# Letting the row adds of one expert run together in the last group of a Mamba + mixture-of-experts kernel

## The chip, the cores and the metric

The kernel runs on one core of a Trainium2 chip. The metric is the device time of one execution in microseconds (us), the median of three executions. The core has five engines that run their own instruction streams and meet only at semaphores: TensorE (PE; its weight loads are shown as PEld), VectorE (DVE), ScalarE (ACT), GpSimd (POOL) and SyncE (SP), which here issues plain DMAs.

## The reference, cut to what matters

A Mamba block works on x of 8 x 1024 tokens of width 256, and then a mixture of 8 experts with the two best experts of each token:

```
logits = x_flat @ router_w + router_b
topk_weights, topk_indices = jax.lax.top_k(router_logits, k=2)
...
ff_gate = jax.lax.ragged_dot(sorted_tokens, we_gate, group_sizes)
ff_up = jax.lax.ragged_dot(sorted_tokens, we_up, group_sizes)
ff_out = jax.lax.ragged_dot(silu(ff_gate) * ff_up, we_down, group_sizes)
output_flat = jnp.zeros_like(x_flat).at[sorted_token_idx].add(ff_out * w)
```

A token stands in the lists of two experts, so two rows are added to its output row, and never two of the same expert.

## The kernel before

The tokens are worked through in 16 pieces of 512 (index q). The Mamba scan of a piece takes 16 slots of a loop over slots `s`, which every engine runs over in its own code. The router of piece q scatters each token's row twice into `sorted_x` in DRAM, which has a region for each expert. Rows are then taken back in tiles of 128 rows of one expert. There are 135 tiles (numbers v = 0 to 134) in 16 groups: 1 tile in the first, 8 in each of the others, and 22 in the last, which takes everything that is left. The last group is v = 113 to 134, and it runs after the scan has ended. Its k-th tile is v = 113 + k.

On the reference's inputs the router's choices fix what the last group holds. Counted from them: experts 0 to 6 have two tiles each, one with 128 rows and one with 44, 74, 29, 23, 10, 95 and 109 rows in this order (v = 113 and 114, 115 and 116, ..., 125 and 126); expert 7 has five full tiles (127 to 131); the last three (132 to 134) are empty and hold only rows with a number past the end of the output.

A late tile v goes through these steps, one slot apart or so: SP loads its 128 rows from `sorted_x` into `xt` (`load_tile`), PE transposes them (L740), ACT copies (`take_xt`, L1012), PE multiplies by gate and up weights (`late_gate_up`, L756), ACT takes a tanh (L1032), DVE makes the product (`activate`, L1235 and L1241), PE turns it (`late_turn`, L765), ACT copies it (`late_take`, L1026), PE multiplies by the down weights (`late_down`, L774), ACT scales the result into `yt` (`take_y`, L1020), and POOL issues an indirect DMA that adds the 128 rows to `out` in DRAM (`add_rows`, L1372). The order of the work on each engine is that of the code under the slot number: in slot s, PE has `late_down` of the tile of slot s-4, `late_turn` of s-3, `late_gate_up` of s-1 and the transpose of s; DVE has `activate` of s-2; POOL the add of s-5.

Semaphore `s_add` counts landed adds by 16. Three waits hang on it: `add_rows` of v waits until all earlier adds have landed; `take_y` of v waits until add v-2 has landed, since `yt` has two buffers (`NY`); `load_tile` of v waits until add v-7 has landed, since `xt` has seven (`NX`):

```
wait(pool, s_add, 16 * v)
wait(act, s_add, 16 * (v - NY + 1))
wait(sp, s_add, 16 * (v - NX + 1))
```

Of the kernel before, what the change touches and what calls it, by code (L numbers as in the profile page):

```python
# [24 lines left out]
J = P // 32  # L25
UN = CC * G
# [7 lines left out]
RW = DM + 2  # L34
NOWHERE = 4.0 * NQ * T
LAST = 3 * NE - 2
# [4 lines left out]
NX, NY = 7, 2  # L41
# [27 lines left out]
ALL = []  # L69
# [7 lines left out]
for g in ALL:  # L77
    for k in range(g.nk):
        assert g.at[k] not in BEGINS and g.at[k] > max(BEGINS, default=-99)
        BEGINS[g.at[k]] = g, k  # L80
TOTAL_SLOTS = ALL[-1].at[-1] + 9


def scattered(s):
# [3 lines left out]
def tiles_in(s, late=None):  # L88

    return [BEGINS[s]] if s in BEGINS and late in (None, s >= LATE_FROM) else []  # L90
# [85 lines left out]
def mamba_moe(nc, x, w_in, w_xp, w_dt, w_out, w_moe, chan, a_log, ln_gb, r_w, r_b, consts, out):  # L176
    with ExitStack() as ctx:
        def sb(name, shape, dt=F32):
            return ctx.enter_context(nc.sbuf_tensor(name, shape, dt))
# [4 lines left out]
        def sem(name):  # L184
            return ctx.enter_context(nc.semaphore(name))
# [20 lines left out]
        REPS = 9222  # L206
# [73 lines left out]
        te = sb("te", [P, 3, LAST], U32)  # L280
        tb = sb("tb", [P, 3, LAST], U32)
        te_pad = sb("te_pad", [P, NE], U32)


        xt = sb("xt", [P, NX, RW])
        xT = sb("xT", [P, 2, DC, P])
        yt = sb("yt", [P, NY, DM])
        th = sb("th", [P, 2, DC, P])
        hT = sb("hT", [P, 2, DC, P])
        hT2 = b_bc[:, 0:2, 0:DM].rearrange("p b (c t) -> p b c t", t=P)  # L290
# [83 lines left out]
        s_ga = sem("s_ga")  # L374
        s_h = sem("s_h")
        s_add = sem("s_add")
        s_token = sem("s_token")
        s_none = sem("s_none")
        s_state = sem("s_state")
# [8 lines left out]
        def wait(eng, s, value):  # L388
            if value > 0:
                eng.wait_ge(s, value)  # L390

        def by_parity(v):

# [22 lines left out]
        def _(sp):  # L416
# [63 lines left out]
            def load_tile(g, k):  # L480
                v = g.tiles + k
                if k == 0:
                    scattered_all(sp, 0, g.q)
                    scattered_all(sp, 1, g.q)
                    sp.wait_ge(s_te, g.q + 1)
                    if g.q == NQ - 1:
                        sp.wait_ge(s_zero, 16 * (NE + 1))
                wait(sp, s_add, 16 * (v - NX + 1))
                at = tile_row(sp, g, k)
                sp.dma_start(xt[:, v % NX, :], sorted_x[bass.ds(at, P), :]).then_inc(s_xt[v % NX], 16)  # L490


            chosen = {}
# [87 lines left out]
        def _(pe):  # L581
# [150 lines left out]
            def late_transpose(g, k):  # L732
                v = g.tiles + k
                pe.wait_ge(s_xt[v % NX], 16 * (v // NX + 1))
                if v == LATE:
                    pe.wait_ge(s_m2, UN * NQ)
                    pe.wait_ge(s_h3, UN * NQ)
                wait(pe, s_xv, v - 1)
                for c in range(DC):
                    last = pe.transpose(dA[:, 2 + v % 2, c * P:(c + 1) * P], xt[:, v % NX, c * P:(c + 1) * P], ident)  # L740
                last.then_inc(s_ta, 1)


# [63 lines left out]
        def _(act):  # L807
# [206 lines left out]
            def take_y(g, k):  # L1014
                v = g.tiles + k
                act.wait_ge(s_td, v + 1)
                if v < LATE:
                    wait(act, s_ta, TOKENS_WITH[v])
                wait(act, s_add, 16 * (v - NY + 1))
                act.activation(yt[:, v % NY, :], p_a[:, DM:2 * DM], ACT.Copy, scale=xt[:, v % NX, DM:DM + 1]).then_inc(s_yv, 1)  # L1020

            def late_take(g, k):
                v = g.tiles + k
# [69 lines left out]
        def _(dve):  # L1093
# [86 lines left out]
            def place(q):  # L1180
# [38 lines left out]
                j = step_of(dve.tensor_tensor(taken[:], some[:, 1:NE + 1], some[:, 0:NE], ALU.subtract))  # L1219
                dve.wait_ge(s_place, i)  # L1220
                dve.wait_ge(s_past, q + 1)
                k = step_of(dve.tensor_tensor(past[:, 0:nk], past[:, 0:nk], step[:].unsqueeze(1).to_broadcast([P, nk, NE + 2]), ALU.mult))
                dve.wait_ge(s_place, j)
                dve.scalar_tensor_tensor(r5[:, QT + 1, :], taken[:], -float(P), r5[:, QT + 1, :], ALU.mult, ALU.add).then_inc(s_state, 1)
                dve.tensor_copy(te[:, g.b, 0:nk], tef[:, 0:nk])
                dve.wait_ge(s_place, k)
                m = step_of(dve.tensor_reduce(tbf[:, 0:nk], past[:, 0:nk], AX_X, ALU.add))
                dve.wait_ge(s_place, m)
                dve.tensor_scalar(tb[:, g.b, 0:nk], tbf[:, 0:nk], float(ZERO_PAGE), None, ALU.min).then_inc(s_te, 1)
                assert done[0] == PL * (q + 1)  # L1230

            def activate(g, k):
                v = g.tiles + k
                dve.wait_ge(s_tanh, v + 1)
                dve.scalar_tensor_tensor(th[:, v % 2], th[:, v % 2], 1.0, gate(g, v), ALU.add, ALU.mult).then_inc(s_ga, 1)  # L1235
                dve.wait_ge(s_ga, v + 1)
                if v < LATE + 2:
                    wait(dve, s_td, v - 1)
                else:
                    dve.wait_ge(s_turn, v - LATE - 1)  # L1240
                dve.tensor_tensor(hT[:, v % 2], th[:, v % 2], up(g, v), ALU.mult).then_inc(s_h, 1)  # L1241

            for s in range(FIRST, TOTAL_SLOTS):
                q, n = s // UN, s % UN
                unit = 0 <= s < UN * NQ
                tail = 0 <= q - 1 < NQ
                if unit:
                    unit_first(s)
                if unit:
                    unit_third(s)  # L1250
                for p in range(NQ):
                    if s == UN * (p + 1) + 8:
                        weights(p)
                        place(p)
                if unit:
                    unit_second(s)
                for g, k in tiles_in(s - 2):
                    activate(g, k)
                if unit:
                    unit_last(s)  # L1260
                if unit and n in (4, 8, 12):
                    gated(q, n // G - 1)
                if tail and n == 0:
                    gated(q - 1, CC - 1)
                if n == 6 and tail:
                    route(q - 1)
                if s == FIRST + 4:
                    tables()

        @block.gpsimd  # L1270
        def _(pool):
# [93 lines left out]
            def add_rows(g, k):  # L1365

                v = g.tiles + k
                pool.wait_ge(s_yv, v + 1)
                pool.wait_ge(s_x2w, 16 * (g.q + 1))
                wait(pool, s_add, 16 * v)  # L1370
                number = xt[:, v % NX, DM + 1:DM + 2].bitcast(U32)
                pool.indirect_dma_start(out=out_rows, out_offset=bass.IndirectOffsetOnAxis(ap=number, axis=0), in_=yt[:, v % NY, :], in_offset=None,  # L1372
                                        bounds_check=NQ * T - 1, oob_is_err=False, compute_op=ALU.add).then_inc(s_add, 16)

            def no_token():
# [90 lines left out]
```

## Time and profile before

| | us |
|---|---|
| median of 3 runs | 2319.36 (2318.93 to 2322.07) |
| profiled execution, its own time | 2327.84 |
| its span in the profile | 2325.9 |
| from the start of add 113 to the start of add 134 | 93.5 |
| granted TensorE clock over the span, as a share of 2.4 GHz | 0.888 |

A row of the timeline has the start of an instruction from the start of the span, its length, engine, line, operation and tiles, and in brackets how long the engine had stood idle and what the profile takes for the releaser. For a DMA, the POOL row is the making of the transfer's descriptors; the chain of waits shows how long it took from there to its landing ("DMA out<-yt,xt").

### The profile page before, as it was taken

How to read it: one execution, taken by the hardware profiler on the slowest of the kernel's cores; microseconds unless marked ns; L12 is line 12 of the kernel's file. 1: busy time of each engine (PE TensorE's matmuls, PEld its weight loads, DVE VectorE, ACT ScalarE, POOL GpSimd, SP SyncE). 2: the span in 40 equal slices, each digit the busy share in tenths (PEclk: the TensorE clock that was granted, in tenths of full speed). 3: DMA queues.
4: the chain of work that ended last, by engine and by line, in shares of the span. 5: the costliest groups of instructions: out<-in, count | busy, mean ns of one | idle time of the engine just before them, and what ended most of it. 6: DMA issues, size and time to landing. Idle time of an engine off the chain costs nothing.

```text
span 2325.9 us, 32531 instructions
## 1 busy us (share of the span) xinstructions
PE 1795.3 (77%) x7694; PEld 923.0 (40%) x7694; DVE 1893.7 (81%) x2437; ACT 1806.5 (78%) x3753; POOL 1933.7 (83%) x1190
## 2 busy tenths in 40 slices
PE   5566768697878788797878788797878788666785
PEld 2112323153534344353434444353434344343542
DVE  0389988899889888899889888899889888999221
ACT  5888888888898788888998788888998787763332
POOL 1588897989999898999999898999999898987333
PEclk9888978797989898998989898997989898786998
DMA  1635454477777786677777786677777786797332
GB/s 57 145 83 141 105 141 109 125 177 184 169 178 178 169 213 160 170 183 184 174 175 180 163 218 157 171 183 180 176 179 178 160 221 147 183 259 221 70 49 34
DMA packets 217979, 369.34 MB, mean 159 GB/s; under 512 B 31040, under 2 KB 86592, under 8 KB 217664
## 3 DMA queue, kind: packets, MB, share of 16 engines
q1 hardware_dynamic: 192208, 333.56, 58.1%
q0 software_dynamic: 25584, 33.71, 7.5%
q8 instruction: 65, 1.06, 0.2%
q14 instruction: 122, 1.00, 0.1%
HBM read 285.05 MB, written 83.01 MB: 158 GB/s over the span
## 4 chain that ended last, share of the span: by engine, by line
issue 23%; POOL 23%; ACT 18%; PE 18%; DVE 9%; DMA 8%; POOLq 0%; ACTq 0%; DVEq 0%; SPq 0%
DMA out<-yt,xt 8%; POOL arena L1324 8%; DVE dA L1116 5%; PE ring L603 5%; ACT dA L979 4%; POOL arena L1332 4%; POOL out L1372 3%; POOL sorted_x L1362 2%; PE yps L697 2%; PE ring L611 2%; DVE arena L1116 2%; POOL arena L1347 2%; POOL arena L1342 1%; PE p_g L729 1%; PE ring L640 1%
## 5 line engine op out<-in xcount | busy, mean ns | idle before, releaser
L1324 POOL TENSOR_TENSOR arena<-arena,b_bc 128x2048 f32<-128x2048 f32 x256 | 998.4, 3900 | 88.3 <-PE yps L697 88.3
L979 ACT ACTIVATE dA<-arena,a_s 128x512 f32<-128x512 f32 x1024 | 680.5, 684 | 116.0 <-DVE arena L1125 69.9
L1116 DVE TENSOR_TENSOR_SCAN dA<-dA,arena 128x512 f32<-128x512 f32 x384 | 454.5, 1213 | 156.8 <-ACT dA L979 107.3
L1116 DVE TENSOR_TENSOR_SCAN dA<-dA,carry,arena 128x512 f32<-128x512 f32 x384 | 477.6, 1274 | 52.3 <-POOL arena L1324 36.2
L697 PE MATMUL yps<-arena,const_s 128*32 128x512 f32 x2048 | 320.4, 702 | 59.9 <-POOL arena L1332 35.9
L1332 POOL TENSOR_TENSOR arena<-arena,c_bc 128x511 f32<-128x511 f32 (+1 forms) x256 | 335.0, 1308 | 28.3 <-DVE arena L1116 26.5
L1125 DVE TENSOR_TENSOR arena<-dA,c_bc 128x1024 f32<-128x1024 f32 x256 | 313.6, 1225 | 8.8
L1372 POOL DMA_INDIRECT out<-yt,xt x135 | 215.0, 1592 | 115.7 <-ACT yt L1020 84.1
L595 PE MATMUL ring<-arena 128*128 128x512 f32 x488 | 265.4, 670 | 55.5 <-ACT arena L883 21.6
L729 PEld LDWEIGHTS p_g<-xT,w_e 128*128 128x128 f32 x1680 | 216.7, 209 | 127.5 <-issue 127.5
L603 PE MATMUL ring<-arena 128*128 128x512 f32 x480 | 236.8, 639 | 35.3 <-ACT arena L883 13.6
L729 PE MATMUL p_g<-xT,w_e 128*128 128x128 f32 x1680 | 236.7, 299 | 20.8 <-issue 11.4
L709 PE MATMUL p_a<-w_e,hT 128*128 128x256 f32 x420 | 128.3, 434 | 112.0 <-ACT xT L1012 80.6
L1138 DVE TENSOR_TENSOR arena<-dA,c_bc 128x512 f32<-128x512 f32 x256 | 176.4, 689 | 5.2
L1116 DVE TENSOR_TENSOR_SCAN arena<-dA,carry,arena 128x512 f32<-128x512 f32 x128 | 163.2, 1275 | 11.3 <-ACT dA L979 11.3
L1116 DVE TENSOR_TENSOR_SCAN arena<-dA,arena 128x512 f32<-128x512 f32 x128 | 155.2, 1213 | 20.6 <-ACT dA L979 20.6
L1362 POOL DMA_INDIRECT sorted_x<-xf,pos x128 | 127.1, 993 | 45.3 <-issue 30.1
L595 PEld LDWEIGHTS ring<-arena 128*128 128x128 f32 x488 | 91.5, 208 | 183.5 <-issue 88.2
L603 PEld LDWEIGHTS ring<-arena 128*128 128x128 f32 x480 | 91.2, 200 | 161.4 <-issue 95.9
L709 PEld LDWEIGHTS p_a<-w_e,hT 128*128 128x128 f32 x420 | 86.0, 216 | 160.4 <-issue 114.6
L697 PEld LDWEIGHTS yps<-arena,const_s 128*32 128x32 f32 x2048 | 43.5, 115 | 229.8 <-issue 177.7
L623 PE MATMUL ring<-w_out_s,sz 128*128 128x256 f32 x512 | 122.7, 382 | 4.7 <-ACT uc L887 3.8
(171 smaller groups left out, 2973.5 us busy)
## 6 DMA issues: line engine op xcount, KB each, us to landing
arena<-dt_d SPq DMA_DIRECT2D x512, 256.0 KB
w_e<-in_w_moe SPq DMA_DIRECT2D x105, 512.0 KB, 4.7
dt_d<-arena SPq DMA_DIRECT2D x128, 256.0 KB, 2.4
w_e<-in_w_moe SPq DMA_DIRECT2D x105, 256.0 KB
xt<-sorted_x SPq DMA_DIRECT2D x135, 129.0 KB
b_bc<-bc_d SPq DMA_DIRECT2D x256, 64.0 KB, 2.4
c_bc<-bc_d SPq DMA_DIRECT2D x256, 64.0 KB, 5.3
xs<-in_x SPq DMA_DIRECT2D x16, 512.0 KB, 4.4
```

Source lines behind the costliest of these rows:

```text
L595: last = pe.matmul(bank(q, name), w_in_s[:, c, ch * P:(ch + 1) * P], xnT[:, c, :], start=c == 0, stop=c == DC - 1)
L603: last = pe.matmul(bank(q, f"W{c}"), d_conv[:, c, k, :], ubuf[:, c % 2, k:k + T], start=k == 0, stop=k == TAPS - 1)
L697: last = pe.matmul(yps[32 * j:32 * j + 32, :], sumsel, hs[:, u % 3, j, :], start=False, stop=g == G - 1, skip_group_check=True)
L709: last = pe.matmul(p_a[:, DM:2 * DM], hT[:, v % 2, c, :], w_e[:, v % 2, col:col + DM], start=c == 0, stop=c == DC - 1)
L729: last = pe.matmul(p_g[:, f, :], w_e[:, v % 2, col:col + P], xT[:, v % 2, c, :], start=c == 0, stop=c == DC - 1)
L979: act.activation(dA[:, j, :], rep_dt[:, c % 2, j, :], ACT.Exp, scale=a_s[:, n, j:j + 1]).then_inc(s_exp, 1)
L1116: return dve.tensor_tensor_scan(out_ap, dA[:, j, :], hs[:, u % 3, j, :], init, ALU.mult, ALU.add)
L1125: dve.tensor_tensor(hs[:, u % 3, 0:2], dA[:, 0:2], c_bc[:, g, :].unsqueeze(1).to_broadcast([P, 2, T]), ALU.mult).then_inc(s_m01, 1)
L1138: dve.tensor_tensor(hs[:, u % 3, 2], dA[:, 2], c_bc[:, g, :], ALU.mult).then_inc(s_m2, 1)
L1324: pool.tensor_tensor(hs[:, u % 3], rep_dtu[:, c % 2], b_bc[:, g, :].unsqueeze(1).to_broadcast([P, J, T]), ALU.mult).then_inc(s_dbu, 1)
L1332: pool.tensor_tensor(hs[:, u % 3, 3, 0:end], hs[:, u % 3, 3, 0:end], c_bc[:, g, 0:end], ALU.mult).then_inc(s_hp, 1)
L1372: pool.indirect_dma_start(out=out_rows, out_offset=bass.IndirectOffsetOnAxis(ap=number, axis=0), in_=yt[:, v % NY, :], in_offset=None, bou ...
```

## The change

For v < 113 nothing changes. For the last group: the rows go into 15 new buffers (`xt_own`) and then into the seven of `xt`, the results into 22 new buffers (`yt_own`), both in parts of `arena` that the scan has left; the loads no longer wait for adds, except that the sixteenth waits once for add 112; `take_y` no longer waits for adds. When the tile table of the last group is made, DVE makes `turn` too: for tile k, 16 times the number of adds up to the first tile of its expert. Before the add of tile k > 0, DVE reads its entry into a register, waits until `s_add` has reached it, and lets POOL go through `s_go`, by a copy of one column. So adds of one expert wait only for the adds up to their expert's first tile.

```diff
+OWN = ALL[-1].tiles
+NEW_ROWS = 15
...
+        def rows_of(v):
+            k = v - OWN
+            return xt[:, v % NX, :] if k < 0 else xt_own[:, k, :] if k < NEW_ROWS else xt[:, k - NEW_ROWS, :]
+
+        def result_of(v):
+            return yt[:, v % NY, :] if v < OWN else yt_own[:, v - OWN, :]
...
-                wait(sp, s_add, 16 * (v - NX + 1))
+                if v < OWN:
+                    wait(sp, s_add, 16 * (v - NX + 1))
+                elif k == 0:
+                    sp.wait_ge(s_dbu, UN * NQ)
+                    sp.wait_ge(s_exp, J * UN * NQ)
+                elif k == NEW_ROWS:
+                    sp.wait_ge(s_add, 16 * OWN)
+                if v >= OWN:
+                    sp.wait_ge(s_xt[v % NX], 16 * (v // NX))
...
-                wait(act, s_add, 16 * (v - NY + 1))
-                act.activation(yt[:, v % NY, :], p_a[:, DM:2 * DM], ACT.Copy, scale=xt[:, v % NX, DM:DM + 1]).then_inc(s_yv, 1)
+                if v < OWN:
+                    wait(act, s_add, 16 * (v - NY + 1))
+                elif k == 0:
+                    act.wait_ge(s_ymm, UN * NQ)
+                act.activation(result_of(v), p_a[:, DM:2 * DM], ACT.Copy, scale=rows_of(v)[:, DM:DM + 1]).then_inc(s_yv, 1)
...
+                if last:
+                    dve.tensor_tensor(past[:, :, 1:NE + 1], past[:, :, 1:NE + 1],
+                                      count_e[:, 1:NE + 1].unsqueeze(1).to_broadcast([P, LAST, NE]), ALU.mult).then_inc(s_order, 1)
+                    dve.wait_ge(s_order, 1)
+                    dve.tensor_reduce(turnf, past[:, :, 1:NE + 1], AX_X, ALU.add).then_inc(s_order, 1)
+                    dve.wait_ge(s_order, 2)
+                    dve.tensor_scalar(turn[:], turnf, 16.0, 16.0 * OWN, ALU.mult, ALU.add).then_inc(s_order, 1)
+
+            def may_add(k):
+
+                if k == 1:
+                    dve.wait_ge(s_order, 3)
+                dve.wait_ge(s_add, dve.value_load(turn[0:1, k:k + 1], min_val=16 * OWN, max_val=16 * TILES))
+                dve.tensor_copy(past2[:, k, 0:1], turnf[:, k:k + 1]).then_inc(s_go, 1)
...
+                for g, k in tiles_in(s - 5, True):
+                    if g.tiles == OWN and k > 0:
+                        may_add(k)
...
-                wait(pool, s_add, 16 * v)
-                number = xt[:, v % NX, DM + 1:DM + 2].bitcast(U32)
-                pool.indirect_dma_start(out=out_rows, out_offset=bass.IndirectOffsetOnAxis(ap=number, axis=0), in_=yt[:, v % NY, :], in_offset=None,
+                if v <= OWN:
+                    wait(pool, s_add, 16 * v)
+                else:
+                    pool.wait_ge(s_go, k)
+                number = rows_of(v)[:, DM + 1:DM + 2].bitcast(U32)
+                pool.indirect_dma_start(out=out_rows, out_offset=bass.IndirectOffsetOnAxis(ap=number, axis=0), in_=result_of(v), in_offset=None,
```

On DVE, in the slots of the last group, there were only the two instructions of `activate` for one tile after another (number, line, operation, and the semaphores it waits for):

```order
2028 L1235 SCALAR_TENSOR_TENSOR th<-th,p_g 128x256 [waits s_tanh]
2029 L1241 TENSOR_TENSOR hT<-th,p_g 128x256 [waits s_turn,s_ga]
2030 L1235 SCALAR_TENSOR_TENSOR th<-th,yps 128x256 [waits s_tanh]
2031 L1241 TENSOR_TENSOR hT<-th,yps 128x256 [waits s_turn,s_ga]
2032 L1235 SCALAR_TENSOR_TENSOR th<-th,p_g 128x256 [waits s_tanh]
2033 L1241 TENSOR_TENSOR hT<-th,p_g 128x256 [waits s_turn,s_ga]
```

Now, from the slot of tile 117's `activate` on (2005 and 2006), a register load, two register operations and a copy of one column stand behind each `activate`; the copy waits for `s_add`:

```order
2005 L1285 SCALAR_TENSOR_TENSOR th<-th,yps 128x256 [waits s_tanh]
2006 L1291 TENSOR_TENSOR hT<-th,yps 128x256 [waits s_turn,s_ga]
2007 L1279 TENSOR_LOAD turn [waits s_order]
2008 L1279 ISA x2
2009 L1280 COPY arena<-arena 128x1 [waits s_add]
2010 L1285 SCALAR_TENSOR_TENSOR th<-th,p_g 128x256 [waits s_tanh]
2011 L1291 TENSOR_TENSOR hT<-th,p_g 128x256 [waits s_turn,s_ga]
2012 L1279 TENSOR_LOAD turn
2013 L1279 ISA x2
2014 L1280 COPY arena<-arena 128x1 [waits s_add]
```

The copy for the add of tile v stands behind `activate` of tile v+3 and ahead of `activate` of tile v+4.

On POOL the end of the program was this, with the eight scatters of piece 15 between the adds of group 14; 27 adds stand at its end, the last five of group 14 and the 22 of the last group:

```order
1094 L1372 DMA out_0<-yt,xt 8192x256 [waits s_add,s_x2w,s_yv] x2
1095 L1362 DMA sorted_x<-xf,pos 66688x258 [waits s_token,s_zero,s_w12,s_pos] x4
1096 L1372 DMA out_0<-yt,xt 8192x256 [waits s_add,s_x2w,s_yv]
1097 L1362 DMA sorted_x<-xf,pos 66688x258 [waits s_swap,s_token,s_zero,s_w12,s_pos] x4
1098 L1372 DMA out_0<-yt,xt 8192x256 [waits s_add,s_x2w,s_yv] x27
```

and is now:

```order
1097 L1415 DMA sorted_x<-xf,pos 66688x258 [waits s_swap,s_token,s_zero,s_w12,s_pos] x4
1098 L1428 DMA out_0<-yt,xt 8192x256 [waits s_add,s_x2w,s_yv] x5
1099 L1428 DMA out_0<-arena 8192x256 [waits s_add,s_x2w,s_yv]
1100 L1428 DMA out_0<-arena 8192x256 [waits s_go,s_x2w,s_yv] x14
1101 L1428 DMA out_0<-arena,xt 8192x256 [waits s_go,s_x2w,s_yv] x7
```

Add 113 still waits for `s_add`; 114 to 134 wait for `s_go`. The order of the adds is the same.

On SP the loads of the last group each waited for `s_add`; now the first (tile 113) waits for the scatters, the table and the scan's end, and each of the next 14 only for the landing of the load seven before it:

```order
1823 L499 TENSOR_LOAD tb [waits s_dbu,s_zero,s_exp,s_te,s_xt1,s_sct11,s_sct01]
1824 L499 ISA x2
1825 L519 ISA
1826 L519 DMA arena<-sorted_x 128x258
1827 L499 TENSOR_LOAD tb [waits s_xt2]
1828 L499 ISA x2
1829 L519 ISA
1830 L519 DMA arena<-sorted_x 128x258
1831 L499 TENSOR_LOAD tb [waits s_xt3]
```

So 15 loads of the last group can be issued one behind the other.

## Rows read from the trace of the kernel before

**Rows 1.** Windows: busy time of each engine, granted clock, DMA share, GB/s.

```profile
2215.00:2228.00 13.00, 12.66 (x51) 7.78 (x51) 3.99 (x10) 5.91 (x18) 3.09 (x2) 1.00 0.32 48
2228.00:2318.00 90.00, 61.33 (x212) 34.65 (x210) 14.53 (x35) 25.62 (x72) 30.84 (x20) 0.92 0.28 43
```

**Rows 2.** The chain of waits: adds of the last group and what stands between them.

```profile
2203.18 3.77 DMA out<-yt,xt
...
2224.82 3.78 DMA out<-yt,xt
2228.68 0.48 ACT yt L1020
...
2229.45 3.65 DMA out<-yt,xt
...
2239.15 3.68 DMA out<-yt,xt
...
2243.69 4.10 DMA out<-yt,xt
...
2248.64 3.06 DMA out<-yt,xt
...
2311.26 2.70 DMA out<-yt,xt
```

**Rows 3.** Timeline of POOL: add 107, behind a scatter, then adds 112, 115, 127 and 134.

```profile
2190.88 1.60 POOL L1372 DMA_INDIRECT out<-yt,xt  x1 [0.30 <-issue]
...
2220.20 1.55 POOL L1372 DMA_INDIRECT out<-yt,xt  x1 [6.14 <-ACT yt L1020]
...
2233.96 1.54 POOL L1372 DMA_INDIRECT out<-yt,xt  x1 [2.96 <-ACT yt L1020]
...
2287.99 1.54 POOL L1372 DMA_INDIRECT out<-yt,xt  x1 [2.98 <-ACT yt L1020]
...
2318.35 1.54 POOL L1372 DMA_INDIRECT out<-yt,xt  x1 [2.00 <-DMA out<-yt,xt]
```

**Rows 4.** Timeline of ACT: results of tiles 111 and 112, tanh of 115 and 117.

```profile
2207.03 0.47 ACT L1020 ACTIVATE yt<-p_a,xt 128x256 f32<-128x256 f32 x1 [4.17 <-DMA out<-yt,xt]
2207.41 0.38 ACT L1012 ACTIVATE xT<-dA 128x256 f32<-128x256 f32 x1
...
2218.95 0.47 ACT L1020 ACTIVATE yt<-p_a,xt 128x256 f32<-128x256 f32 x1
...
2220.89 0.38 ACT L1032 ACTIVATE th<-yps 128x256 f32<-128x256 f32 x1
...
2226.93 0.38 ACT L1032 ACTIVATE th<-yps 128x256 f32<-128x256 f32 x1
```

**Rows 5.** Timeline of DVE: a small cast, and `activate` of tile 115.

```profile
2184.82 0.16 DVE L1205 CAST pos<-posf 128x8 uint32<-128x8 f32 x1
...
2221.30 0.42 DVE L1235 SCALAR_TENSOR_TENSOR th<-th,yps 128x256 f32<-128x256 f32 x1 [2.15 <-ACT th L1032]
2221.75 0.42 DVE L1241 TENSOR_TENSOR hT<-th,yps 128x256 f32<-128x256 f32 x1
```

**Rows 6.** Timeline of PE: the turning of tile 115.

```profile
2224.30 0.38 PE L765 MATMUL dA<-const_s,hT 128*128 128x128 f32 x2
```

**Rows 7.** One tile load of SP, step by step (ns min/median/max).

```profile
L478 SPq TENSOR_LOAD <-tb x28: 269/274/681, 2165.0 to 2291.9; - x28
L478 SPq FUSED_REGOPS  x28: 152/152/156, 2165.3 to 2292.2; - x28
...
L490 SPq DMA_DIRECT2D xt<-sorted_x x22: 215/338/347, 2200.5 to 2292.6; - x22
```

**Rows 8.** Chain of waits, and window, of one add beside the scan's traffic.

```profile
1126.58 5.90 DMA out<-yt,xt
...
1126.00:1132.00 6.00, 6.00 (x33) 4.25 (x32) 5.44 (x5) 5.51 (x13) 5.85 (x5) 1.00 1.09 222
```

**Rows 9.** DMA queue of SP from 2206 to 2212 us (packets, MB, share of 16 engines): one tile load.

```profile
q1 hardware_dynamic: 144, 0.13, 8.4%
```

More of the change, by code:

```diff
@@ L282, in mamba_moe @@
         te_pad = sb("te_pad", [P, NE], U32)
+        turn = sb("turn", [P, LAST], U32)
         xt = sb("xt", [P, NX, RW])
@@ L287, in mamba_moe @@
         yt = sb("yt", [P, NY, DM])
+        FREE = 6 * DM * NE
+        xt_own = lies(FREE, NEW_ROWS, RW)
+        past2 = lies(FREE + NEW_ROWS * RW, LAST, NE + 2)
+        turnf = lies(FREE + NEW_ROWS * RW + LAST * (NE + 2), LAST)
+        yt_own = lies(REPS + 4 * J * T, LAST, DM)
+        assert FREE + NEW_ROWS * RW + LAST * (NE + 3) <= REPS + 4 * J * T and LAST * DM <= 3 * J * T
         th = sb("th", [P, 2, DC, P])
@@ L376, in mamba_moe @@
         s_add = sem("s_add")
+        s_order = sem("s_order")
+        s_go = sem("s_go")
         s_token = sem("s_token")
@@ L487, in load_tile @@
                         sp.wait_ge(s_zero, 16 * (NE + 1))
-                wait(sp, s_add, 16 * (v - NX + 1))
+                if v < OWN:
[7 more added lines that the diff above has]
+                    sp.wait_ge(s_xt[v % NX], 16 * (v // NX))
                 at = tile_row(sp, g, k)
-                sp.dma_start(xt[:, v % NX, :], sorted_x[bass.ds(at, P), :]).then_inc(s_xt[v % NX], 16)
+                sp.dma_start(rows_of(v), sorted_x[bass.ds(at, P), :]).then_inc(s_xt[v % NX], 16)
             chosen = {}
@@ L739, in late_transpose @@
                 for c in range(DC):
-                    last = pe.transpose(dA[:, 2 + v % 2, c * P:(c + 1) * P], xt[:, v % NX, c * P:(c + 1) * P], ident)
+                    last = pe.transpose(dA[:, 2 + v % 2, c * P:(c + 1) * P], rows_of(v)[:, c * P:(c + 1) * P], ident)
                 last.then_inc(s_ta, 1)
@@ L1221, in place @@
                 dve.wait_ge(s_past, q + 1)
-                k = step_of(dve.tensor_tensor(past[:, 0:nk], past[:, 0:nk], step[:].unsqueeze(1).to_broadcast([P, nk, NE + 2]), ALU.mult))
+                starts = past2 if last else past
+                if last:
+                    dve.wait_ge(s_dbu, UN * NQ)
+                    dve.wait_ge(s_exp, J * UN * NQ)
+                k = step_of(dve.tensor_tensor(starts[:, 0:nk], past[:, 0:nk], step[:].unsqueeze(1).to_broadcast([P, nk, NE + 2]), ALU.mult))
                 dve.wait_ge(s_place, j)
@@ L1226, in place @@
                 dve.wait_ge(s_place, k)
-                m = step_of(dve.tensor_reduce(tbf[:, 0:nk], past[:, 0:nk], AX_X, ALU.add))
+                m = step_of(dve.tensor_reduce(tbf[:, 0:nk], starts[:, 0:nk], AX_X, ALU.add))
                 dve.wait_ge(s_place, m)
@@ L1230, in place @@
                 assert done[0] == PL * (q + 1)
+                if last:
+                    dve.tensor_tensor(past[:, :, 1:NE + 1], past[:, :, 1:NE + 1],
[9 more added lines that the diff above has]
+                dve.tensor_copy(past2[:, k, 0:1], turnf[:, k:k + 1]).then_inc(s_go, 1)
             def activate(g, k):
```

## The prediction, made before the changed kernel ran

> **What bounds the kernel now.** I read the windows first. From 2215 to 2228 us the last group's tiles flow with PE busy for 12.66 of 13 us; from 2228 to 2318 no engine is full (PE 61.33 of 90, DVE 14.53) and the DMA engines are busy for 0.28 of the time [rows 1]. So something serial holds the last 90 us. The chain of waits names it: it runs from one add's landing to the next [rows 2]. Add 113 starts at 2224.82 and lands 3.78 later, at 2228.60; add 114 starts at 2229.45, 0.85 later. The ACT row at 2228.68 between them is a bystander: it is `take_y` of tile 115, which had waited for the same landing. It gives one useful price, 0.08 us from a landing to the next instruction of a waiting engine. One tile costs about 3.7 + 0.85 us, and from add 115 to add 127 twelve tiles took 2287.99 - 2233.96 = 54.03 us [rows 3], 4.5 each.
>
> The next limit below it is PE. Undisturbed, the tanh of tiles 115 and 117 start at 2220.89 and 2226.93 [rows 4]: 3.02 us a tile. What 3.02 instead of 4.5 would save at most over 21 adds is some 31 us.
>
> **The change, part by part.** Before add 113 nothing in the order of adds changes, and add 113 still waits for add 112. From then on there are two regimes.
>
> *Prices.* From a landing to the next expert's first add the way is now landing, DVE's copy, POOL: 0.08, a copy of one column, and POOL's reaction. For the copy I take the small cast's 0.16 [rows 5]. POOL's reaction is 0.78, from `take_y` of tile 112 (2218.95 + 0.47) to its add at 2220.20 [rows 3, 4]. The sum is 1.02, instead of 0.85: the new link costs 0.17 at each boundary. A second add of the same expert needs only POOL: 1.54 for the descriptors and the 0.30 that stands ahead of an unhindered indirect DMA, 1.84 [rows 3]. DVE is quicker than that: two instructions of `activate`, 0.87 [rows 5], a register load with its operations, 0.27 + 0.15 by SP's rows [rows 7], and the copy, 1.6 in all. DVE's own register load is in no row; its bounds are nothing, where it is hidden, and SP's longest, 0.68.
>
> *The pairs, tiles 114 to 126.* Add 114's permission stands behind `activate` of tile 117. That starts 0.41 after its tanh (2220.89 to 2221.30 for tile 115 [rows 4, 5]), at 2227.34; with 0.87, 0.42, 0.16 and 0.78 the add starts at 2229.6, and before at 2229.45: the same, and I keep 2229.45. It lands 3.65 later. Add 115, the first of expert 1, follows at 2234.12. Then each pair costs 1.84 to its second add, that one's landing, and 1.02. The landings are 3.68 for 116, and I take this for 124 and 126 too, and 3.06 for 118, with 29 rows, and for 120 and 122 [rows 2]. Six pairs: 6 x 2.86 + 3 x 3.68 + 3 x 3.06 = 37.38, so add 127 starts at 2271.50 instead of 2287.99. The first add of a pair starts 1.84 earlier and lands within 4.10, the longest row [rows 2], so mostly earlier than the second.
>
> *Is DVE's wait in the way of the tiles behind it?* This is the cost to look for: `may_add` of tile v blocks `activate` of v+4. Undisturbed, `activate` of tile 115 ends at 2222.17 [rows 5] and PE turns the tile at 2224.30 [rows 6]: 2.1 us of slack. Undisturbed, `activate` of tile v starts at 2227.34 + 3.02 x (v - 117). For 121 that is 2239.4, and the permission before it comes at 2239.9; for 131 it is 2269.6, and the permission comes at 2270.7, 1.1 late. All the others lie between. So no blocked `activate` uses up the slack, and PE keeps its 3.02. If boundaries were dearer by more than about 0.2 us each, the slack would be gone at the end of the pairs, and every further 1 us would be 1 us of the result.
>
> *Expert 7 and the empty tiles.* Now the compute leads: add 128 stands behind `activate` of tile 132, which ends at 2227.34 + 15 x 3.02 + 0.87 = 2273.5; with 0.42, 0.16 and 0.78, add 128 starts at 2274.9. Then 129 at 2277.9, 130 at 2280.9. No `activate` is left, so 131 follows by 1.84 at 2282.8 and lands at 2286.6 (3.78). The three empty tiles wait for it: 132 at 2287.6, 133 and 134 by 1.84 each, 134 at 2291.3. It lands in 2.70, as an empty tile does [rows 2], at 2294.0. Before, that was 2318.35 + 2.70 = 2321.05. **This part is worth 27.0 us.**
>
> *The loads.* Tile loads leave the adds behind and come in one burst: 15 loads, one every 0.77 us by SP's steps [rows 7], from 2200.5 to about 2212, and each takes 8.4% of 6 us, 0.5 us, of every DMA engine [rows 9]. In this burst lie adds 108 (2198.41) and 109 (2203.18 [rows 2]); add 109's landing frees ACT for the result of tile 111 at 2207.03, behind which tile 112's copy at 2207.41 stands [rows 4], and with it the start of the whole group. Beside the scan's traffic, with the DMA engines full, an add took 5.90 instead of 3.77 [rows 8]. The burst fills 0.5/0.77 of the engines and the adds need some of the rest, so it is nearer to full than to empty only for part of the time; bounds are 0 and 2 x 2.1 = 4.2, and I take 0.8. Later loads meet little. The burst's gain, rows that are there earlier, is nothing: PE waits for no rows worth naming here.
>
> The Trainium skill ("DMA: Bandwidth & Descriptors", section "Queues, rings and completion order") says that a DMA's semaphore increment lands only after all earlier writes of that DMA engine, across its queues, so a landing would also wait for load writes queued before it. The trace's 5.90 agrees in direction [rows 8]; the sum would take the upper bound, 4.2, instead of 0.8.
>
> *The rest at nothing.* The three table instructions on DVE (under 1 us) run at about 2187, ahead of an `activate` whose result PE doesn't want for 2 us; if that cover were gone they would cost at most that 1 us, once. The waits for `s_dbu`, `s_exp` and `s_ymm` are for the scan, which has ended. The copies of one column queue ahead of `activate` only.
>
> The same skill (same page, section "Latency and other measured facts") gives about 600 ns as the floor of a `tensor_load`; SP's rows show 0.27 [rows 7], so the trace disagrees. By the page DVE's step would be 0.33 longer: still under POOL's 1.84 in a pair, and 0.33 once for expert 7.
>
> **The sum.** 27.0 - 0.8 = 26.2 us. The profiled execution took 2327.84 and would take 2301.6; the median stands 8.5 us lower, and I take the difference over: 2319.36 - 26.2 = 2293.2.
>
> **The rivals.**
> - *Slower landings side by side* (0.20). No row before shows two adds in flight. If the second one's transfer queued behind the first's, it would land later by what an add takes after its descriptors, some 2.1 less the 0.3 by which it starts later: 1.8. Six pairs cost 10.8 more, of which the slack still absorbs 1.0: gain 26.2 - 9.8 = 16.4, or 2303.0. With 4.2 from the burst it is 13.0. For it speaks [rows 8]; against it, that the DMA engines stand idle for 0.72 of this time [rows 1] and that the adds of a pair are 1.84 apart.
> - *The change doesn't do what it says* (0.04): in effect one add at a time, for instance because DVE's order lets a second permission out only when its pair's landing has passed. Then 21 steps cost 0.17 more each: +3.6 us, 2323, within 0.2%. Against it: DVE needs only 1.6 us between two permissions.
> - *Slower* (0.04): two adds in flight hinder each other in DRAM so much that a pair is dearer than serial. A pair costs 9.0 now (54.03/6); 1.84 + landing + 1.02 passes it once the second add's landing is over 6.1 us. At 8.0, pairs cost 10.9, 11 us more over six; the run of expert 7 and the empties, 30.4 us from add 127 to 134 before, would still save about 6: 5 us slower, 2324. The longest landing in this stretch is 4.10 [rows 2].
> - *As forecast* (0.72): its own range is a gain of 23 to 28, 2291 to 2296.
>
> **How the numbers follow.** The range runs from 2290, with the burst at nothing and a tile or two quicker, to 2303, the first rival's time; beyond lie its worse half and the two last cases. About 0.2% (4.6 us) is what a measurement can tell from no change. Faster 0.92 (the forecast and the first rival), same 0.04, slower 0.04.
>
> **What would show it.** In the profile after: adds of a pair 1.9 us apart and the next pair's first about 1.0 after the landing; add 127 near 2272, 128 to 130 spaced by 3.0, the last add near 2292; the chain of waits through DVE's L1280 in the pairs and through PE in expert 7; `take_y` waiting for PE only. The prediction is wrong if PE waits for DVE's product in the pairs (slack overdrawn), if landings of second adds are over 4 us, or if the row of tile 112's copy moves from 2207.4 to later than 2209.

## The result, and the profile after

The changed kernel took 2297.94 us (median of 4 runs) against 2320.72 before; the ratio is 0.9887, with a 95% interval of 0.9864 to 0.9909. By the interval that is a gain of 21 to 32 us; the two medians differ by 22.8. Predicted were 26.2 and 2293.2 us. The profiled execution's span is 2297.1 us instead of 2325.9. (One of the six executions of the repeat below took 5806.81 us, for a reason that no run shows; its ratio leaves this one out.)

The adds first, in the timeline of POOL after the change (columns as in [rows 3]). The rows are adds 113 to 119, then 127 to 132, and 134; L1428 is the indirect DMA of `add_rows`:

```profile
2224.17 1.54 POOL L1428 DMA_INDIRECT out<-arena  x1 [3.08 <-DMA out<-yt,xt]
2229.07 1.54 POOL L1428 DMA_INDIRECT out<-arena  x1 [3.36 <-DVE arena L1280]
2233.82 1.54 POOL L1428 DMA_INDIRECT out<-arena  x1 [3.21 <-DVE arena L1280]
2235.67 1.54 POOL L1428 DMA_INDIRECT out<-arena  x1 [0.30 <-issue]
2241.63 1.54 POOL L1428 DMA_INDIRECT out<-arena  x1 [4.42 <-DVE arena L1280]
2243.47 1.54 POOL L1428 DMA_INDIRECT out<-arena  x1 [0.30 <-issue]
2247.64 1.54 POOL L1428 DMA_INDIRECT out<-arena  x1 [2.62 <-DVE arena L1280]
...
2272.60 1.54 POOL L1428 DMA_INDIRECT out<-arena  x1 [3.14 <-DVE arena L1280]
2274.44 1.54 POOL L1428 DMA_INDIRECT out<-arena,xt  x1 [0.30 <-DVE arena L1280]
2276.29 1.54 POOL L1428 DMA_INDIRECT out<-arena,xt  x1 [0.30 <-issue]
2278.46 1.54 POOL L1428 DMA_INDIRECT out<-arena,xt  x1 [0.63 <-issue]
2280.99 1.54 POOL L1428 DMA_INDIRECT out<-arena,xt  x1 [0.99 <-ACT arena L1052]
2285.84 1.54 POOL L1428 DMA_INDIRECT out<-arena,xt  x1 [3.30 <-DVE arena L1280]
...
2289.53 1.54 POOL L1428 DMA_INDIRECT out<-arena,xt  x1 [0.30 <-issue]
```

A pair is now visible as a pair: 2233.82 and 2235.67, with "0.30 <-issue" ahead of the second, which waited for nothing. The first add of the next expert has DVE's copy (L1280) as its releaser. From add 113 to add 134 it is 65.36 us; before it was 93.53 [rows 2, 3].

On DVE the permission for add 119, the first of expert 3, and then `activate` of tile 123, which had stood blocked behind it, and the permission for the pair's second add:

```profile
2246.62 0.15 DVE L1280 COPY arena<-arena 128x1 f32<-128x1 f32 x1 [3.92 <-DMA out<-arena]
2246.69 0.41 DVE L1285 SCALAR_TENSOR_TENSOR th<-th,yps 128x256 f32<-128x256 f32 x1
2247.13 0.42 DVE L1291 TENSOR_TENSOR hT<-th,yps 128x256 f32<-128x256 f32 x1
2247.77 0.16 DVE L1280 COPY arena<-arena 128x1 f32<-128x1 f32 x1 [0.21 <-issue]
```

From the copy's start to the add at 2247.64 it is 1.02 us, and with 0.08 from the landing 1.10. The second permission comes 1.15 behind the first, well under POOL's 1.84, and the register load (L1279; ns min/median/max) is nearly as short as SP's [rows 7]:

```profile
L1279 DVEq TENSOR_LOAD <-turn x21: 296/303/542, 2227.2 to 2285.5; - x21
```

The chain of waits has turned over. Before, it went from landing to landing [rows 2]. After, the profile follows PE from tile 112 on, one turning, gate and up multiplication, transpose and down multiplication behind the other, and meets the adds only at add 131 (start, length, what):

```profile
2206.66 0.38 ACT xT L1041
...
2276.71 1.72 PE p_g L785 x4
2278.43 0.86 PE p_a L803 x4
2279.29 0.23 PE dA L794 x2
...
2279.83 0.48 ACT arena L1052
2280.30 0.69 issue
2280.99 3.80 DMA out<-arena,xt
...
2284.82 0.15 DVE arena L1280
```

The link into add 131 has to be read with care. The profile names the ACT row that came last before it, 2279.83, but that is the result of tile 132. Results that read `xt` (of tiles 128 and later) start at 2267.20, so the fourth of them, tile 131's, is the row at 2277.03, which ended 3.5 us ahead of the add. What add 131 waited for is its permission: the copy at 2279.97 stands behind `activate` of tile 134, and the add follows it by 1.02 us, as at every boundary. In the repeat below it is 1.02 too (2268.29 and 2269.31).

```profile
2267.20 0.47 ACT L1052 ACTIVATE arena<-p_a,xt 128x256 f32<-128x256 f32 x1
...
2277.03 0.47 ACT L1052 ACTIVATE arena<-p_a,xt 128x256 f32<-128x256 f32 x1
...
2279.83 0.47 ACT L1052 ACTIVATE arena<-p_a,xt 128x256 f32<-128x256 f32 x1
```

```profile
2279.34 0.42 DVE L1291 TENSOR_TENSOR hT<-th,p_g 128x256 f32<-128x256 f32 x1
2279.97 0.15 DVE L1280 COPY arena<-arena 128x1 f32<-128x1 f32 x1 [0.22 <-DMA out<-arena,xt]
```

`activate` of tile 134 in its turn waits for PE and the tanh. So the end of the last group is now paced by compute, through DVE's place in the order, and the add chain of the pairs runs beside it, nearly as long. The windows say the same: PE is busy for 57.44 of 66 us, where it was 61.33 of 90 [rows 1].

```profile
2224.00:2290.00 66.00, 57.44 (x225) 34.89 (x223) 18.10 (x59) 27.02 (x76) 32.86 (x22) 0.98 0.33 45
```

### The profile page after: what moved, and what is told of

Same layout as the page of the kernel before. It is cut to its first block, busy times and chain, and to the rows that moved or that the text cites. A ratio compares the mean times of both kernels' runs of the same rounds, so it can differ in the third digit from the quotient of the medians.

```text
span 2297.1 us, 32600 instructions
## 1 busy us (share of the span) xinstructions
PE 1789.8 (78%) x7694; PEld 921.0 (40%) x7694; DVE 1896.2 (83%) x2461; ACT 1807.2 (79%) x3753; POOL 1933.9 (84%) x1190
## 4 chain that ended last, share of the span: by engine, by line
PE 24%; issue 22%; POOL 21%; ACT 20%; DVE 8%; DMA 4%; POOLq 0%; ACTq 0%; DVEq 0%; SPq 0%
POOL arena L1377 6%; ACT dA L1008 5%; POOL arena L1385 4%; DVE dA L1148 4%; PE ring L632 4%; DMA out<-yt,xt 3%; PE ring L624 3%; POOL out L1428 3%; PE yps L726 3%; POOL sorted_x L1415 2%; PE ring L640 2%; DVE arena L1148 2%; POOL arena L1400 2%; ACT L1008 1%; ACT L945 1%
## 5 line engine op out<-in xcount | busy, mean ns | idle before, releaser
L1428 POOL DMA_INDIRECT out<-yt,xt x113 | 181.0, 1602 | 55.1 <-ACT yt L1052 28.2
```

## The experiments

Executions of one kernel scatter by some 10 to 15 us here, and so does the time at which add 113 starts (2213.8 to 2226.8 us in these profiles, though the kernels are all but the same up to there). So I read each profile by stretches of the add chain, and take the clock's ratio beside it. Times are the starts of the adds on POOL, in us; each row is one profiled execution:

| kernel | 109 to 113 | 113 to 115 | 115 to 127 | 127 to 134 | 113 to 134 | ratio to before (95%) |
|---|---|---|---|---|---|---|
| before | 21.64 | 9.14 | 54.03 | 30.36 | 93.53 | |
| changed | 22.11 | 9.65 | 38.78 | 16.93 | 65.36 | 0.9887 (0.9864 to 0.9909) |
| again | 21.97 | 9.44 | 37.71 | 16.73 | 63.88 | 0.9865 (0.9839 to 0.9891) |
| own_serial | 21.75 | 9.70 | 53.59 | 30.38 | 93.67 | 0.9998 (0.9984 to 1.0013) |
| one_at_a_time | 21.70 | 10.10 | 56.98 | 31.52 | 98.60 | 1.0026 (1.0011 to 1.0041) |
| static_table | 21.85 | 6.77 | 36.28 | 17.96 | 61.01 | 0.9872 (0.9850 to 0.9894) |
| sp_permits | 21.99 | 6.41 | 38.84 | 16.07 | 61.32 | 0.9866 (0.9844 to 0.9888) |
| earlier | 21.77 | 7.00 | 37.93 | 17.27 | 62.20 | 0.9865 (0.9840 to 0.9890) |
| later | 21.66 | 12.56 | 38.91 | 15.94 | 67.41 | 0.9887 (0.9860 to 0.9913) |
| paced_loads | 21.65 | 10.00 | 38.14 | 16.79 | 64.93 | 0.9885 (0.9861 to 0.9909) |
| dear_permit | 21.85 | 11.28 | 40.63 | 17.86 | 69.77 | 0.9906 (0.9884 to 0.9929) |
| empties | 21.69 | 9.39 | 37.24 | 14.44 | 61.07 | 0.9852 (0.9825 to 0.9879) |
| sp_empties | 23.57 | 6.40 | 38.54 | 14.95 | 59.89 | 0.9849 (0.9824 to 0.9874) |

**again.** The changed kernel once more, with no edit.

> The changed kernel once more, to narrow its gain. The two traces stand 28.8 us apart in their spans, the medians 22.8. If the traces show all of it, five more rounds give a gain of 26 to 29 us; if the new kernel is slower when it isn't profiled, the gain stays near 23.

2293.62 against 2324.52 us, a gain of 30.9, and by the interval 25 to 37. That is somewhat above the 26 to 29 that were expected if the traces showed all of it. The stretches of the two profiles show gains of 28.2 and 29.7 us from add 113 to 134, so the first 22.8 was low by scatter of the total, as far as the overlapping intervals can tell. The second profile is 1.5 us shorter from add 113 to 134, and 1.3 us of this has a cause that the trace shows: in the first, PE stood still three times behind a late permission (see "DVE's block and PE's slack" below).

**own_serial.** The buffers without the concurrency:

```diff
-                if v <= OWN:
-                    wait(pool, s_add, 16 * v)
-                else:
-                    pool.wait_ge(s_go, k)
+                wait(pool, s_add, 16 * v)
...
-                for g, k in tiles_in(s - 5, True):
-                    if g.tiles == OWN and k > 0:
-                        may_add(k)
```

> The buffers alone: own row and result buffers and unhindered loads, but every add waits for all earlier ones, and no permissions. Theory (the adds' own chain was the bound, not the buffers): no change against the kernel before, within 0.2%; the adds stay 4.5 us apart. Rival (the waits of take_y and of the loads were part of the chain): up to 5 us faster.

No change, 0.9998, and the same 93.67 us. The buffers and the freed waits of `take_y` and the loads are worth nothing by themselves: the ACT rows in the chain before [rows 2] were bystanders. The whole gain is the adds' own chain. No run lets adds run together without the own buffers, so it isn't shown whether they are needed for it.

**one_at_a_time.** The detour without the concurrency:

```diff
-                dve.wait_ge(s_add, dve.value_load(turn[0:1, k:k + 1], min_val=16 * OWN, max_val=16 * TILES))
+                dve.wait_ge(s_add, 16 * (OWN + k))
```

> Permissions through DVE, but each add waits for all earlier ones. It prices the detour alone. Theory: 0.17 us more for each of 21 adds than in the kernel before, 97 us from add 113 to add 134, and 3 to 4 us slower than before, or no change by the clock. Rival (blocked activates stall PE on top): over 100 us.

98.60 us, 4.9 more than with `own_serial`, or 0.23 for each of 21 adds, and slower than before by 0.1 to 0.4%. Expected were 97 us, the rival had over 100. So the detour itself costs, and somewhat more than the 0.17 that was reckoned. Its chain of landings is so long that DVE's blocked `activate` does reach PE here (who waited for whom, us in total, times, longest):

```profile
PE dA L794 <- DVE hT L1291: 13.4, 15, 2.2
```

That is 13.4 us of PE's time, but PE was not the bound here, and the detour's price explains the longer stretch without it. The changed kernel's own list has no such row; its blocked `activate` reaches PE in another way, told below.

**static_table.** POOL waits on constants and DVE is out of it:

```diff
+FIRST_OF = [0, 0, 2, 2, 4, 4, 6, 6, 8, 8, 10, 10, 12, 12, 14, 14, 14, 14, 14, 19, 19, 19]
...
-                    pool.wait_ge(s_go, k)
+                    pool.wait_ge(s_add, 16 * (OWN + FIRST_OF[k]))
...
-                for g, k in tiles_in(s - 5, True):
-                    if g.tiles == OWN and k > 0:
-                        may_add(k)
```

> POOL waits on constants, the table worked out beforehand for these inputs; DVE gives no permissions and is never blocked. Theory (DVE's place in the order sets the start of the pairs and of the last adds): add 114 starts about 3 us earlier, near 1.84 behind add 113; a boundary costs 0.85 instead of 1.0; PE has no gaps left, and the end is set by the result of tile 131, so the last add starts some 1.5 us earlier than in the changed kernel. Rival (DVE's detour costs the whole chain): 3 us at the start and 0.15 at each of 7 boundaries reach the end, 4 us.

Add 114 follows 113 by 1.84 us, where it was 4.90 in both profiles of the changed kernel:

```profile
2217.51 1.54 POOL L1426 DMA_INDIRECT out<-arena  x1 [3.15 <-DMA out<-yt,xt]
2219.35 1.54 POOL L1426 DMA_INDIRECT out<-arena  x1 [0.30 <-issue]
```

The pairs take 36.28 us, 1.4 less than with "again": six boundaries at 0.24 less. That is the detour's price again, by another way. But of the 4.1 us gained by add 127 only 2.9 are left at add 134 (61.01 against 63.88), since add 131 now waits for the result of tile 131, which doesn't come sooner: it starts 52.71 us behind add 113, instead of 55.55 behind the permission in "again". The theory had this limit right and its worth wrong: it reckoned with 1.5 us, as if add 131 of the changed kernel waited for its result too. Against the first profile (65.36) the gain is 4.35, so by the number alone the rival's 4 isn't out; it is out by the 1.2 us that are lost between add 127 and the end.

**sp_permits.** The same permissions with the table made on the chip, but given by SP:

```diff
+            def sp_may_add(k):
+                if k == 1:
+                    sp.wait_ge(s_order, 3)
+                sp.wait_ge(s_add, sp.value_load(turn[0:1, k:k + 1], min_val=16 * OWN, max_val=16 * TILES))
+                sp.sem_inc(s_go, 1)
```

Its calls stand behind SP's loads of the slot, and those of `may_add` on DVE are left out.

> SP, idle at the end but for the loads, reads the table and gives the permissions, between the loads; DVE gives none. Theory (the detour is cheap, its place on DVE is what costs): as with the table of constants, 61 us from add 113 to add 134 instead of 64 to 65, add 114 within 2.5 us of add 113, a boundary at 0.9 to 1.1. Rival (the register load and the wait for a register are dear wherever they stand): 64 us or more.

61.32 us, as with the constants; expected was 61. Add 131 starts 52.90 us behind add 113, set by its result as in static_table. So what is dear isn't the table but where the permission stands. The pairs alone took 38.84 us, 2.6 more than with the constants; most of this stands at two adds, 116 and 124, whose landings were late (5.54 and 5.32 us to the next add, where the kernels with DVE's permissions mostly have 4.7), and it was gone by add 131.

**earlier** and **later.** The permission one slot sooner (behind `activate` of v+2), or one slot later:

```diff
-                for g, k in tiles_in(s - 5, True):
+                for g, k in tiles_in(s - 4, True):
...
-                for g, k in tiles_in(s - 5, True):
+                for g, k in tiles_in(s - 6, True):
```

> Each permission one slot earlier on DVE, behind activate of tile v+2 and ahead of v+3. Theory (slack of 2.1 us): add 114 starts 3 us earlier; but a blocked activate is now needed 3 us sooner, so PE waits some 1 to 2 us at each boundary and gives the 3 us back: 62 to 67 us from add 113 to 134, with PE waiting for DVE's product at most boundaries. Rival (blocking never matters): 61 us, as with the constants.

> Each permission one slot later on DVE, behind activate of tile v+4. Theory (place in DVE's order counts): add 114 starts 3.0 us later, the pairs follow shifted by that, add 130 stands behind the last activate and 131 1.84 behind it; the last add starts 2.5 to 3.5 us later than in the changed kernel. Rival (landings alone pace the adds): the same as the changed kernel within 1 us, since DVE is idle for most of the time.

Later came out nearly as expected: add 115 starts 2.9 to 3.1 us later, add 134 2.1 to 3.5. Earlier was a miss in part. Add 114 starts 1.85 behind 113, as expected, and 62.20 us lies in the expected range, but PE doesn't stand still at most boundaries, only at two; its row for the gaps ahead of the gate multiplication is this (the second number is how often):

```profile
PE p_g L785 <- issue: 0.4, 2, 0.3
```

By the starts of the tanh the two gaps cost 0.95 us together, and not 1 to 2 at each boundary. I had overlooked that the landings move with the permission: add 115 starts 2.4 to 2.7 us sooner too, so in the pairs the blocked `activate` is hardly nearer to its deadline than before.

**paced_loads.** No burst of loads:

```diff
                 if v >= OWN:
                     sp.wait_ge(s_xt[v % NX], 16 * (v // NX))
+                    sp.wait_ge(s_xv, v - 3)
```

> The changed kernel with no burst: a load of the last group waits until three tiles before it are taken by ACT. Theory (the burst costs little): add 109 lands in 3.8 instead of 4.15 us, add 116 in 3.7 instead of 4.9; the last add 0 to 1.5 us earlier, not told by the clock. Rival (the burst holds back the start by up to 4.2 us, the prediction's bound): 3 to 4 us faster than the changed kernel.

Add 109 lands in 3.85 instead of 4.15 us, each from its own chain of waits (paced_loads first, then the changed kernel):

```profile
2205.10 3.85 DMA out<-yt,xt
```

```profile
2202.06 4.15 DMA out<-yt,xt
```

From add 109 to add 113 it takes 21.65 us, as it did before (21.64); the kernels with the burst took 21.66 to 22.11, but for sp_empties, which has its own reason (below). So the burst costs 0 to 0.5 us, not 0.8, and by far not 4.2. Add 116 was expected to land in 3.7 us and took 3.9. The last add came 0.4 us sooner than in the first profile of the changed kernel and 1.0 later than in the second, which two profiles can't tell from no change. So the rival's 3 to 4 us are out.

**dear_permit.** One more pass of DVE ahead of each permission:

```diff
+                dve.tensor_scalar(t_s[:], t_s[:], 1.0, None, ALU.mult).then_inc(s_order, 1)
+                dve.wait_ge(s_order, 3 + k)
                 dve.tensor_copy(past2[:, k, 0:1], turnf[:, k:k + 1]).then_inc(s_go, 1)
```

> Ahead of every permission DVE passes once over a tile of 128x512 (its values unchanged), some 0.3 to 0.7 us. Theory (the pairs are a chain, the expert run is not): each of seven boundaries is that much dearer, and nearly all of it reaches the end, since PE's slack is used up by then: 67 to 69 us from add 113 to add 134. Rival (the compute behind PE sets the end, landings are hidden): 65 us, as in the changed kernel.

The pass takes 0.43 us (ns min/median/max):

```profile
L1280 DVE TENSOR_SCALAR t_s<-t_s x21: 426/428/543, 2227.0 to 2289.9; 128x512 f32<-128x512 f32 x21
```

From add 113 to 134 it is 69.77 us, 4.4 more than in the changed kernel's one profile and 5.9 more than in its other. The theory's 67 to 69 is nearer than the rival's 65: a dearer boundary reaches the end. The way it takes can be read from the tanh: the later permissions let PE stand still seven times ahead of a gate multiplication, 4.8 us in all, where "again" has 0.04. These 4.8 us, the 0.43 of the pass ahead of the permission for add 131, and 0.66 more from add 131 to 134 make up the 5.9.

**empties** and **sp_empties.** The three empty tiles add nothing, so they need not wait for expert 7; the table's sum leaves out one column, once with DVE's and once with SP's permissions:

```diff
-                    dve.tensor_reduce(turnf, past[:, :, 1:NE + 1], AX_X, ALU.add).then_inc(s_order, 1)
+                    dve.tensor_reduce(turnf, past[:, :, 1:NE], AX_X, ALU.add).then_inc(s_order, 1)
```

> The changed kernel, but the table leaves out the end of expert 7, so that the three empty tiles, which add nothing, wait for no add of expert 7. Theory: add 132 starts 1.84 behind add 131 instead of 4.6 to 4.9; 61 to 62.5 us from add 113 to add 134, 2.9 us off the end. The landing of 131 is the later one then, so of these 2.9 us some 2.6 are left: add 134 starts 3.7 behind 131 and lands 2.7 later, at 6.4, behind 131's own 3.8. Rival (three adds side by side with 131 slow each other): no gain.

> SP gives the permissions and the empty tiles don't wait for expert 7: both gains together, 58 to 59 us from add 113 to add 134, 3 us faster than with SP alone and 5 to 6 faster than the changed kernel; the clock may tell it only just. Rival: the result of tile 134 comes too late, and the end is that of PE: 60 us or more.

61.07 and 59.89 us from add 113 to 134. From add 127 on it is 14.44 and 14.95 instead of 16.7 to 16.9. With DVE, 61 to 62.5 were expected, and add 132 starts 1.85 behind 131 as expected; add 134 stands three such steps behind 131, 5.55 us, and not the 3.7 of the expectation. With SP, expected were 58 to 59, and 59.89 lies between this and the rival's 60; it is 1.4 less than with sp_permits and not 3. The results of the last tiles are in the way, as the rival said; these are adds 131 to 134:

```profile
2277.29 1.54 POOL L1435 DMA_INDIRECT out<-arena,xt  x1 [0.55 <-issue]
2280.09 1.54 POOL L1435 DMA_INDIRECT out<-arena,xt  x1 [1.26 <-ACT arena L1062]
2282.47 1.54 POOL L1435 DMA_INDIRECT out<-arena,xt  x1 [0.83 <-ACT arena L1062]
2284.35 1.54 POOL L1435 DMA_INDIRECT out<-arena,xt  x1 [0.34 <-issue]
```

From add 109 to 113 sp_empties took 23.57 us, 1.6 more than sp_permits, because TensorE's granted clock stayed at its lower level (1.2 GHz) for one gate multiplication more. It took 3.76 us there, while in the other profiles the one at this place, the second behind the wait for tile 112's rows, took 1.98 to 2.00 (the multiplication, then the window with the granted clock third from the end):

```profile
2210.49 3.76 PE L795 MATMUL yps<-arena,xT 128*128 x4 [0.56 <-ACT xT L1051]
```

```profile
2210.00:2214.20 4.20, 3.71 (x6) 1.54 (x7) 0.84 (x2) 0.63 (x2) 1.54 (x1) 0.51 0.29 35
```

By the measured totals, sp_empties at 0.9849 (2292.27 against 2325.18 us) is the best of all ratios, but its interval overlaps that of the changed kernel's repeat, so that it is the faster one is shown by the stretch from add 113 to 134 alone, and not by the total.

## Why the prediction was right, and where its steps were off

**The bound and its kind: right.** A serial chain of landings held the last 90 us, and the buffers' waits were not part of it (own_serial, 0.9998). Of what was tried, only letting adds run together pays.

**The price of a boundary: 1.02 reckoned, 1.10 measured.** The missing 0.08 lies behind the copy: POOL's reaction was 0.78 behind ACT's result, and is 0.87 behind DVE's copy (2247.64 - 2246.77). Against the 0.85 of before the detour costs 0.25 instead of 0.17, and static_table (0.24) and one_at_a_time (0.23) agree.

**The pairs: 37.38 reckoned from add 115 to 127, 38.78 and 37.71 measured.** Gap 1.84, as reckoned. A second add in flight mostly lands as fast as one alone: 3.66 for add 124 (2261.31 to the next permission at 2265.05, less 0.08) and 3.07 for the short 118 (2243.47 to 2246.62), where one alone took 3.68 and 3.06 [rows 2]. The first rival, where every second add lands 1.8 us later, and the slower one are thereby out. Single landings do come late: add 116 took 4.86 in the first profile, over the 4 us that the prediction had named as a sign of being wrong, and 3.65 in the repeat. The ten profiles with adds side by side have 60 pairs behind add 115 on, and in five of them the next pair's first add came 5.3 to 6.0 us behind the second add instead of 3.8 to 5.2 (changed kernel 116, later 122, sp_permits 116 and 124, sp_empties 124). The longest landing in the kernel before was 4.10 [rows 2]. Why these came late, and whether the concurrency has a part in it, stays open.

**DVE's block and PE's slack: the cost was looked for in the right place, but the slack is 1.35 us and not 2.1.** The prediction took the slack from the end of `activate` to PE's turning of the tile. Here is what happened around tile 121 in the changed kernel, whose `activate` stood behind the permission for add 117, held up by the late landing of add 116 (tanh of tiles 121, 122 and 123, then `activate` of 121, then PE's register load with the expert number of tile 123 between 2241.3 and 2242.0 us (ns min/median/max, first and last start), then that tile's gate and up multiplication):

```profile
2238.36 0.38 ACT L1064 ACTIVATE th<-yps 128x256 f32<-128x256 f32 x1
2241.39 0.38 ACT L1064 ACTIVATE th<-p_g 128x256 f32<-128x256 f32 x1
2244.96 0.38 ACT L1064 ACTIVATE th<-yps 128x256 f32<-128x256 f32 x1
```

```profile
2240.68 0.41 DVE L1285 SCALAR_TENSOR_TENSOR th<-th,yps 128x256 f32<-128x256 f32 x1
2241.12 0.42 DVE L1291 TENSOR_TENSOR hT<-th,yps 128x256 f32<-128x256 f32 x1
```

```profile
L778 PEldq TENSOR_LOAD <-te x1: 297/297/297, 2241.6 to 2241.6; - x1
```

```profile
2242.45 1.98 PE L785 MATMUL yps<-arena,xT 128*128 x4 [0.29 <-issue]
```

`activate` started 1.91 us later than its tanh would have let it (2238.36 + 0.41). The tanh of 123 came 3.57 behind that of 122 instead of 3.02: 0.55 lost. PE's queue had stood at the wait ahead of the turning until the product was there at 2241.54, and the register load behind it, which is otherwise made in good time, came only then. The multiplication needs that number, so it, and not the turning, sets the deadline. The profile calls such a gap "issue", which is why no wait for DVE's product is listed. The same difference shows wherever a gap stands behind one blocked `activate`:

| profile, blocked tile | `activate` late by | PE loses | difference |
|---|---|---|---|
| changed, 121 | 1.91 | 0.55 | 1.36 |
| changed, 129 | 1.62 | 0.28 | 1.34 |
| changed, 131 | 1.83 | 0.49 | 1.34 |
| again, 131 | 1.39 | 0.04 | 1.35 |
| dear_permit, 121 | 2.70 | 1.35 | 1.35 |
| dear_permit, 129 | 2.50 | 1.14 | 1.36 |

By the prediction's own sum the latest `activate` is 1.1 late, so PE keeps its 3.02 even so, with 0.25 us to spare instead of 1.0. In the repeat this held. In the first profile one late landing used up the rest: PE lost 1.3 us in three gaps, one of them in the pairs, which the prediction had named as a sign of being wrong, and add 131 started 56.82 us behind add 113 instead of 55.55. Static_table, sp_permits, own_serial and empties have no such gap.

**Expert 7 and the empties: the failed step.** The prediction says "add 128 stands behind `activate` of tile 132". By its own rule, and by the order shown ahead of it, the permission of v stands behind `activate` of v+3, so add 128 stands behind that of 131. I had counted one tile too far. With the right tile the sum reads: add 128 by 1.84 behind 127, 129 by 1.84 again at 2275.2, 130 at 2277.9, 131 at 2280.9, 132 at 2285.7, 134 at 2289.4. That is 64.6 us from add 113, where 65.36 and 63.88 were measured and the prediction had 66.5. It would have made the term 28.9 instead of 27.0 us; the profiles show 28.2 and 29.7. In both profiles add 129 came 1.85 behind 128, as close as POOL can follow, 130 came 2.17 behind 129, and 131 came 2.53 behind 130, on its permission. The place of that permission, behind `activate` of tile 134, is worth 2.8 us: in static_table and sp_permits, where add 131 waits for its result, it starts 52.7 and 52.9 us behind add 113 instead of 55.55.

**The loads' burst: mechanism right, price too high.** 0 to 0.5 us instead of 0.8. The burst itself was slower than reckoned: the 15 loads were issued one every 1.15 us and not every 0.77, up to 2215.5 (start of the first, time to the end of the last issue):

```profile
2199.36 16.43 SPq L519 DMA_DIRECT2D arena<-sorted_x  x15
```

Rows of a landing beside DMA engines that are full (5.90, [rows 8]) say little of one beside engines that are two thirds full. By the Trainium skill's rule ("DMA: Bandwidth & Descriptors", section "Queues, rings and completion order") a landing waits for load writes queued ahead of it, and the estimate by it was 4.2, if they delayed the landing as the scan's traffic had. The trace agrees in direction, 4.15 against 3.85 us for add 109, but shows 0.5 at most.

**The register load.** The Trainium skill's floor of some 600 ns (same page, section "Latency and other measured facts") doesn't hold in these runs: the medians are 303 ns on DVE and 274 on SP.

The two errors have the same sign: a term that was 1.9 too small, and 0.3 to 0.8 too much taken off for the burst. Without them the sum is 28.4 to 28.9 us. From add 109 to 134 the profiles show 27.7 and 29.3, so 26.2 was 1.5 to 3.1 us too low. By the measured totals it was 22.8 (21 to 32) at first and 30.9 (25 to 37) in the repeat. That the forecast lies between these two is in part luck: the first is 3.4 us below it and the second 4.7 above. And 2297.94 us misses the forecast's own narrow range of 2291 to 2296, as does its gain of 22.8 that of 23 to 28, while both lie inside the wide range, whose other end was meant for the first rival.

## What to carry to other kernels

When a chain of DMA landings bounds a stage, more buffers alone give nothing; find which of the transfers really exclude each other, and let only those wait. A wait that an in-order engine takes on another's behalf costs three times: its hop at each link (0.25 us here); its place in that engine's order, which was worth more here (3.05 us at add 114 and 2.8 at add 131); and the work queued behind it, once it is held longer than its consumer can bear (1.35 us here). Put it on an engine with nothing urgent queued behind. A consumer's deadline is that of its whole queue, the register load behind the wait too, and not that of the instruction that reads the data. Before summing along such an order, write down for one late item which instruction stands ahead of it, and check it against the order: one tile off was 1.9 us.

## What the runs showed of the hardware that was not expected

Two adding indirect DMAs in flight on one core, 1.84 us apart, mostly land as fast as one by itself (3.66 against 3.68, 3.07 against 3.06 us); in 5 of 60 pairs the second was late, by up to 1.2 us in the changed kernel (4.86). A register load behind a wait delayed the multiplication that needs its number, in a gap that the profile puts down to "issue" (2241.6 and 2242.45 above). And the time up to the last group differs by up to 13 us between profiled executions of kernels whose code up to there is all but the same (add 113 starts at 2213.8 to 2226.8 us), while the stretch from add 113 to 134 differs by 1.5 us between the two profiles of the changed kernel: for a change in one stage the stretch tells more than the total.
